# First attention of a vision tower: whole transfers of queries and keys, split products, row norms on 32-column tiles

## What is computed

```python
t = layernorm(h)                      # 32 x 257 x 256
q, k, v = split_heads(t @ Wq, t @ Wkv)     # 16 heads; q and k 16 wide, v 64 wide
q, k, v = l2norm(q), l2norm(k), l2norm(v)
attn = square(relu(q @ k.T))
out = tanh_norm(attn @ v)             # tanh(|o|) * o / |o|
h = h + merge_heads(out) @ Wout
```

## Time and profile before

| what | value |
|---|---|
| median of 3 runs | 3128.6 us (3127.97 to 3133.56) |
| the profiled execution, its own time | 3139.85 us |
| its span, first to last instruction | 3138.1 us |
| mixer and first attention | up to about 1630 us of the span |
| DMA traffic, whole span | 223.12 MB, mean 71 GB/s |

### The profile page before, as it was taken

How to read it: one execution, slowest core, us unless ns; L and a number is a source line. 1 busy time by engine, 2 the same in 40 slices (tenths; PEclk the granted TensorE clock), 3 DMA queues, 4 the chain that set the end, 5 groups by cost and what they waited for, 6 DMA issues and landing times. The chain is left out here.

```text
span 3138.1 us, 66657 instructions
## 1 busy us (share of the span) xinstructions
PE 2907.1 (93%) x21548; PEld 2217.3 (71%) x21549; DVE 2098.8 (67%) x5372; ACT 1442.7 (46%) x2948; POOL 1157.0 (37%) x966
## 2 busy tenths in 40 slices
PE   3899999999999999999966999999999972999998
PEld 1677777777777777777744666666766652999997
DVE  4577677677677777777734777777777855444444
ACT  0444544545545545445422555555555533444443
POOL 3324434434434334334321233333233324444443
PEclk7899999999999999999987999999999985999999
DMA  3424424424424424324302111111111101554544
GB/s 83 96 70 92 107 66 95 107 62 98 102 62 104 98 66 104 94 70 104 87 22 51 49 47 53 43 42 52 45 54 47 44 33 44 77 76 76 77 77 69
DMA packets 161126, 223.12 MB, mean 71 GB/s; under 512 B 30305, under 2 KB 125730, under 8 KB 161074
## 3 DMA queue, kind: packets, MB, share of 16 engines
q1 hardware_dynamic: 135138, 187.50, 23.9%
q0 software_dynamic: 25936, 34.95, 7.2%
HBM read 125.26 MB, written 97.08 MB: 71 GB/s over the span
## 5 line engine op out<-in xcount | busy, mean ns | idle before, releaser
L66 POOL TENSOR_TENSOR vrn<-vsm,inv_root 128x16 f32<-128x16 f32 x64 | 243.8, 3809 | 285.8 <-DVE vsm L836 285.8
L665 ACT ACTIVATE R<-psA 128x1024 f32<-128x1024 f32 x256 | 262.4, 1025 | 168.4 <-PE psA L1150 164.2
L857 DVE TENSOR_TENSOR PR<-R 128x1024 f32<-128x1024 f32 x256 | 321.3, 1255 | 0.0
L2512 POOL DMA_INDIRECT out_rows<-e_y,e_dest x137 | 213.7, 1560 | 289.8 <-DMA out_rows<-e_y,e_dest 182.2
L1904 DVE TENSOR_REDUCE m_nm<-psC 128x4 f32<-128x1028 f32 (+1 forms) x256 | 239.0, 956 | 72.0 <-PE psC L2177 71.4
L1165 PE MATMUL psA<-PR,V 128*64 128x258 f32 x2048 | 283.4, 398 | 0.0
L670 ACT ACTIVATE oTs<-psA 128x258 f32<-128x258 f32 x256 | 99.1, 387 | 358.1 <-PE psA L1165 352.3
L1783 ACT ACTIVATE m_PT<-psC 128x770 f32<-128x770 f32 x256 | 194.0, 810 | 137.3 <-PE psC L2205 137.3
L1210 PE MATMUL psA<-wout,OT 128*128 128x256 f32 x1024 | 244.6, 382 | 0.4 <-DVE OT L899 0.4
L1698 POOL DMA_INDIRECT xg<-tn,idx x124 | 124.5, 1004 | 318.6 <-DMA xg<-tn,idx 186.6
L1210 PEld LDWEIGHTS psA<-wout,OT 128*128 128x128 f32 x1024 | 188.7, 191 | 24.6 <-DVE OT L899 0.7
(11 more groups left out here) (417 smaller groups left out, 7633.0 us busy)
## 6 DMA issues: line engine op xcount, KB each, us to landing
ks<-kparts SPq DMA_DIRECT2D x256, 128.0 KB, 3.3
qs<-qparts SPq DMA_DIRECT2D x256, 128.0 KB, 3.8
e_x<-xg SPq DMA_DIRECT2D x143, 129.0 KB
xraw<-in_x SPq DMA_DIRECT2D x66, 256.0 KB
qparts<-qh SPq DMA_DIRECT2D x128, 128.0 KB, 2.4
kparts<-kh SPq DMA_DIRECT2D x64, 128.0 KB, 2.5
kparts<-kl SPq DMA_DIRECT2D x64, 128.0 KB, 2.4
qparts<-ql SPq DMA_DIRECT2D x64, 128.0 KB, 2.4
```

Of the source, the lines that this page charges most:

```text
L66: return pool.tensor_tensor(out, x, e.to_broadcast(list(out.shape)), ALU.pow)
L665: act.activation(R[:, p % 2].rearrange("p a t n -> p t a n"), ps[:, 0:2, :].rearrange("p t (a n) -> p t a n", a=2), ACT.Relu).then_inc(rel ...
L857: dve.tensor_tensor(PR[:, p % 2, :, :, 0:L], R[:, p % 2], R[:, p % 2], ALU.mult).then_inc(prob_done, 1)
L2512: pool.indirect_dma_start(out, bass.IndirectOffsetOnAxis(ap=dest[:, b % XD:b % XD + 1], axis=0), y[:, b % XD], None, compute_op=ALU.add).t ...
```

## The change

- Queries and keys are computed by three float32r products instead of one float32 product: `load_constants` splits wqk into wqkh and wqkl (two DVE instructions of 128x1024, eight more ACT copies), and `project` has 24 matmuls instead of 8. `project_keys` now waits for xl instead of xT, and `token_lows` moves on DVE to just after `prob 5`, ahead of `result`.
- The ten stores of 128 KB are five of 256 KB, each a whole tile. A load reads pieces of 1 KB instead of 4 KB. The stores of the rounded parts wait only for these.
- `key_sums` and `query_sums` go. `row_norms` (after `project_values(j, 1)`) makes the sums of both on four tiles of 32 columns. A new ACT copy `norm_rows` (after `values(j, 1)`) takes them, `turn_norms` (where `key_sums` stood) turns them with 32 columns, and one lift and one inverse on DVE (`row_inverses`, where `key_norms` stood) serve both.
- `psq` is `prl`'s own memory now, and the copied norms share `osums`.

```diff
+            dve.tensor_copy(wqk_hi[:], wqk0[:]).then_inc(wqk_high, 1)
+            dve.wait_ge(wqk_high, 1)
+            dve.tensor_tensor(wqk_lo[:], wqk0[:], wqk_hi[:].bitcast(F32), ALU.subtract).then_inc(wqk_high, 1)
...
+            dve.memset(v.ind8[:, 8:32], 0.0)
+            dve.tensor_copy(v.sel32[:].rearrange("p (g m) -> p g m", g=4),
+                            v.ident[:].rearrange("p (g r) -> p g r", g=4)[:, :, 0:8])
...
+            def keep_part(part, rows, n, out):
+                sp.dma_start(rows[:, n], part[:].bitcast(F32).rearrange("p c n -> p (c n)")).then_inc(out, 16)
+
+            def heads(rows, hh, n, c):
+                return rows[hh, n:n + 2].rearrange("a (r m) (c n) -> c (a r) m n", m=4, c=KT)[c]
...
                 if c == 0:
+                    sp.wait_ge(k_sq, j + 1)
+                    keep_part(kh, v.kparts, 0, k_out)
                     sp.wait_ge(kl_done, j + 1)
-                    keep_parts((kh, kl), v.kparts, k_out)
+                    keep_part(kl, v.kparts, 1, k_out)
+                    sp.wait_ge(q_sq, j + 1)
+                    keep_part(qh, v.qparts, 0, q_out)
+                    keep_part(qh, v.qparts, 2, q_out)
                     sp.wait_ge(ql_done, j + 1)
-                    keep_parts((qh, ql, qh), v.qparts, q_out)
-                    sp.wait_ge(k_out, 64 * j + 64)
+                    keep_part(ql, v.qparts, 1, q_out)
+                    sp.wait_ge(k_out, 32 * j + 32)
                     lay_out_keys(0, moved0)
...
+            def norm_rows(j):
+                act.wait_ge(norms_summed, j + 1)
+                act.activation(nsums[:], ps[:, BCLS, 0:L], ACT.Copy).then_inc(norms_copied, 1)
...
+            def row_inverses(j, e):
+                dve.wait_ge(norms_turned, j + 1)
+                dve.tensor_scalar(qkm[:], ps[:, BCLS, NORMS:NORMS + 64].rearrange("p (t w g) -> p w t g", t=LT, w=2),
+                                  L2_EPS ** 2, None, ALU.max).then_inc(qk_lift, 1)
+                dve.wait_ge(qk_lift, j + 1)
                 need(dve, v_c, 2 * j)
-                dve.reciprocal(rk[:], km[:]).then_inc(k_inv, 1)
+                dve.reciprocal(qkr[:, e], qkm[:]).then_inc(qk_inv, 1)
...
                     for k in range(KT):
-                        last = pe.matmul(ps[:, bank, c * L:(c + 1) * L], v.wqk[:, k, first + c * P:first + (c + 1) * P],
-                                         xT[:, k, :], start=k == 0, stop=k == KT - 1)
+                        pe.matmul(sums, v.wqkh[:, k, cols], xh[:, k, :], start=k == 0, stop=False)
+                        pe.matmul(sums, v.wqkl[:, k, cols], xh[:, k, :], start=False, stop=False)
+                        last = pe.matmul(sums, v.wqkh[:, k, cols], xl[:, k, :], start=False, stop=k == KT - 1)
                 last.then_inc(done, 1)
...
+            def row_norms(j):
+                pe.wait_ge(k_sq, j + 1)
+                pe.wait_ge(q_sq, j + 1)
+                for w, sq in enumerate((qsq, ksq)):
                     for c in range(2):
+                        g = 2 * w + c
+                        last = pe.matmul(ps[32 * g:32 * g + 32, BCLS, 0:L], v.ind8[:], sq[:, c, :], start=True, stop=True,
+                                         skip_group_check=True)
+                last.then_inc(norms_summed, 1)
+
+            def turn_norms(j):
+                pe.wait_ge(norms_copied, j + 1)
+                for t in range(LT):
+                    col = NORMS + 32 * t
+                    last = pe.matmul(ps[:, BCLS, col:col + 32], nsums[:, t * P:(t + 1) * P], v.sel32[:], start=True,
+                                     stop=True, skip_group_check=True)
+                last.then_inc(norms_turned, 1)
 
             def class_products(j):
-                pe.wait_ge(k_lift, j + 1)
+                pe.wait_ge(qk_lift, j + 1)
+                pe.wait_ge(xT_done, j + 1)
...
                 if more:
                     project_values(j, 1)
+                    row_norms(j)
                 attend(i, d, 5)
                 sim(i, 7)
                 if more:
-                    key_sums(j)
+                    turn_norms(j)
                     project_values(j, 2)
                     project_values(j, 3)
                     class_products(j)
                 attend(i, d, 6)
-                if more:
-                    query_sums(j)
                 attend(i, d, 7)
```

More of the change, by code:

```diff
@@ L225, in _ @@
                 act.activation(v.ewT[:, s, :], ps[:, s, 0:L], ACT.Exp).then_inc(ew_done, 1)
+            act.wait_ge(wqk_high, 2)
+            for k in range(KT):
+                for h in range(2):
+                    for e in range(2):
+                        act.activation(by_half(v.wqkl[:, k])[:, h, e], by_head(wqk_lo[:, k])[:, h, e], ACT.Copy)
         @block.vector
@@ L687, in front @@
                 values(j, 1)
+                norm_rows(j)
                 values(j, 2)
@@ L975, in sample @@
                 prob(i, d, 5)
+                if more:
+                    token_lows(j)
                 if before:
@@ L979, in sample @@
                 if more:
-                    token_lows(j)
                     key_lows(j)
@@ L1112, in project_values @@
                 last.then_inc(v_done, 1)
[L1114 to L1124 removed]
+            def row_norms(j):
+                pe.wait_ge(k_sq, j + 1)
+                pe.wait_ge(q_sq, j + 1)
+                for w, sq in enumerate((qsq, ksq)):
+                    for c in range(2):
+                        g = 2 * w + c
[4 more added lines that the diff above has]
+                pe.wait_ge(norms_copied, j + 1)
+                for t in range(LT):
+                    col = NORMS + 32 * t
+                    last = pe.matmul(ps[:, BCLS, col:col + 32], nsums[:, t * P:(t + 1) * P], v.sel32[:], start=True,
+                                     stop=True, skip_group_check=True)
+                last.then_inc(norms_turned, 1)
             def class_products(j):
[L1127 removed]
+                pe.wait_ge(qk_lift, j + 1)
+                pe.wait_ge(xT_done, j + 1)
                 for k in range(KT):
@@ L1135, in class_products @@
                 last.then_inc(cls_done, 1)
-            def query_sums(j):
-                pe.wait_ge(q_sq, j + 1)
-                pe.wait_ge(racl_done, j + 1)
-                norm_sums(qsq, QN).then_inc(qn_done, 1)
             def sim(i, p):
```

123 lines of the change are left out of this document (51 added, 72 removed).

## The result

| | before | after |
|---|---|---|
| median of 4 runs | 3128.28 us (3125.87 to 3133.56) | 3793.31 us (3788.31 to 3794.37) |
| ratio, with its 95% interval | | 1.212 (1.210 to 1.214) |
| profiled execution, own time and span | 3139.85 us, 3138.1 us | 3794.31 us, 3792.5 us |

The forecast was 3119.3 us in a range of 3106 to 3133, and it is wrong by 674 us. One sample takes 68.20 us from one `sim 0` to the next (1006.13 to 1074.33), where the kernel before took 47.3 us per sample.

What follows compares the result with a forecast made beforehand. Bound: PE's gapless work from `attend 0` to the last values, then a 10.4 us ACT, DVE, POOL chain to the next `attend 0`. Terms -0.65 + 0.07 + 0.28 = -0.30 us, times 31: 3128.6 - 9.3 = 3119.3 us, range 3106 to 3133.

Steps and rivals of the forecast that it cites:

- the DMA term: SP's stores and loads: five whole stores issued at 0.65 us each, 1.3 if by bytes; loads 3 us sooner; cost nothing.
- The bound of 1.3 us: Upper figure for one whole 256 KB store on SP if its issue goes by bytes, instead of 0.65 us.
- The next to be late would be `sim 0`: Where late loads would show first on PE, once the 3 us by which loads were expected sooner were used up.
- the prediction's own signs of being wrong: 10.4 us distance to `attend 0` shrinks; PE idles at `project_keys`, `class_products` or `sim 0`; over two clock falls, 140 to 1560 us.
- The rival with the finer loads: Load issue grows with its pieces, to 1.7 us each, making `sim 0` some 5 us late: 3280 us, chance 0.05.
- split projections: Query and key projections, ahead of the chain: 24 float32r products at 0.117 us save 0.65 us per sample, bounds 0.34 to 0.95.
- wait for xl and joint norms: Ahead of the chain, per sample: `project_keys` waits 0.07 us for xl; `row_norms` and `turn_norms` replacing `key_sums` add 0.28.
- `query_sums`, in the chain's shadow: About 1.0 us of PE inside the chain's stretch; removing it only makes PE wait at `attend 0`, gaining nothing.
- the work done once: `load_constants` adding 1.6 us and sample 0's shorter DMA issue returning 1 to 2: together 0, bounds -1 and +2.
- PE's idle time: Before `attend 0`: grows from nearly nothing to about 1.2 us per sample, released by DVE's PR or POOL.
- The rival of the falling clock: PE's wait at `attend 0` brings more clock falls, 1.4 us each; one every second sample gives 3141 us; chance 0.09.
- PE alone as the bound: All PE savings count, -1.30 us per sample over 31 samples: -40 us, 3088 us; chance 0.08.

Runs made afterwards that it cites:

- experiment 5: Experiment 4's kernel plus five end-of-queue 256 KB stores with 2, 4, 8, 16 and 32 steps in DRAM's first run: 3144.7 us; transfers 6.2, 4.3, 2.5, 1.3, 0.8 us.
- experiment 3: Kernel before with its ten 128 KB stores in the new DRAM layout and loads in 1 KB pieces: 3138.04 us, ratio 1.0021.
- experiment 4: Changed kernel with whole stores whose DRAM first run has 32 steps instead of 2, six stores instead of five: 3120.86 us, ratio 0.9966.
- experiment 7: Experiment 4's kernel with eight idle 8-column products per sample between `attend 6` and `attend 7`: 3121.01 us.
- experiment 10: Experiment 4's kernel with the old norms (`key_sums`, `query_sums`, two lifts, two inverses), split projections kept: 3137.28 us, ratio 1.0022.
- experiment 1: Changed kernel with each 256 KB store cut into two of 128 KB, all else kept: 3122.06 us, ratio 0.997.
- experiment 11: Experiment 6's kernel with the old norms (`key_sums`, `query_sums`, two lifts, two inverses): 3108.25 us, ratio 0.9926.
- experiment 6: Experiment 4's kernel with `turn_norms` and `attend 5` moved behind the last values on PE, DVE and ACT: 3079.0 us, ratio 0.984.

## Why the prediction was wrong

**The step that failed is the DMA term**, "A whole store has 128 pieces of 2 KB: 0.65 too, 1.3 if it goes by bytes. ... Bytes are the same. Cost nothing". It priced the issue and took the transfer for given. The issue did take 0.5 to 0.6 us, for as long as SP could go ahead; the transfer took some 5.2 us on 2 engines instead of the 1.3 us or less that experiment 5 shows on 16. The bound of 1.3 us was a bound on the wrong quantity. "The next to be late would be `sim 0`" named the right place: there the 3 us of cover were gone and 19.9 us more. Idle time at `sim 0` was also one of the prediction's own signs of being wrong. The rival with the finer loads named `sim 0` and a loss too, but by another mechanism; with the finer loads alone the cost was 8 us (experiment 3). What it would have taken was to look at the order of the dimensions in `rows[:, n]` and not only at the size of the pieces: the Trainium skill's rule, page and section above, names the engines from it, and two engines at the 25 GB/s each that the run shows give 5.2 us per store. It was not weighed.

**The other terms held in sum**, on the base of experiment 4, which is the change without that fault:

| term, us per sample | forecast | measured |
|---|---|---|
| split projections | -0.65 | -0.64 (period 47.70 to 47.06) |
| wait for xl and joint norms | +0.07, +0.28 | +0.38 (47.32 to 47.70, samples at full clock) |
| `query_sums`, in the chain's shadow | 0 | 0 (experiment 7) |
| sum | -0.30 | -0.26 (47.32 to 47.06) |
| the run | -9.3 us | -9.3 us (3130.11 to 3120.86) |

That the run comes out at exactly -9.3 is in part luck. It holds some 2 us for the two clock falls that the kernel before has between 140 and 1560 us and the base has not; against that, the base reaches the same point of an early sample 1.3 us later (its second acl starts at 151.58 instead of 150.27), where the prediction had put the work done once at 0. The norms' size is less sure than the table says: with split projections they cost 0.48 by experiment 10 (period 46.58 without a fall, 47.06 on the base). The 0.38 less these 0.48 leave -0.10 for the wait for xl and all else, where the forecast had +0.07; PE never waits for xl on the base. So the row norms were put 0.2 too low, at the upper bound of 0.5, and the rest 0.17 too high, and the two nearly cancel.

**PE's idle time** before `attend 0`, forecast at about 1.2, is 1.03, and the 10.4 us from the end of the last values to `attend 0` are 10.4 still (1037.63 to 1048.06 in one sample of the base). In the kernel after, this wait is gone, since the stall at `sim 0` comes first and the chain ends in its shadow. The same at small size in experiment 1: PE waits 13.6 us for loads at `sim 0`, its wait before `attend 0` is 16.1 instead of 31.0, and the run is 1.2 us longer, less than a measurement tells. That is why the finer loads cost almost nothing there.

**The rival of the falling clock** gave the wrong cause: PE's wait before `attend 0` brought no falls on the base (0 between 140 and 1560 us). Most falls came behind 8-column products between `attend 6` and `attend 7`: 2 in the kernel before, 3 with the idle ones of experiment 7, 25 with `query_sums` beside split projections in experiment 10. The same `query_sums` in the order of experiment 11 brought none. A wait of PE can go with a fall all the same: two of the four in experiment 3 came at one, at `sim 0`. **PE alone as the bound** is false for this order of work and true for that of experiment 6, which at 3079 us is 1.6% faster than the kernel before and the best version here.

## What to carry to other kernels

Before a transfer is made larger, read the instruction's own dimensions on both sides: the same bytes in the same pieces went over 2 engines or 16 by whether the outermost one was 2 or 32. Look for a busy share of the DMA engines that stays at a small number of sixteenths (0.13 here) while someone waits. And an engine that is 99% busy may still hide free room: find the chain that ends with it, and start that chain sooner before shortening work beside it.

## What the hardware showed that was not expected

- Slow transfers seem to hold up their issuing queue: behind two stores under way the next two issues took 8.46 us together and the one after them 5.48, and the loads of the keys stood behind the stores of the queries. On 16 engines each issue took 0.6 us.
- The granted clock can lock in: 25 falls in 25 samples, each 3.4 us long and 1.22 us dear, began at 381 us, after some six samples without one.
- GpSimd's power of 128x16 takes 3809 ns in the mean before, 3490 in the base and 3118 in experiment 6, with the same operands. In the base the one that starts the chain still takes 3.80 us, the other of the sample 3.19. What slows it was not tried.
